# A causal mask added by the matrix engine instead of selected by GpSimd, and another ranking of the work, in a two-layer transformer kernel

## The reference, cut to what matters

```python
q = _rope(q, THETA); k = _rope(k, THETA)
scores = jnp.einsum('bhqd,bhkd->bhqk', q, k) * scale
causal = jnp.tril(jnp.ones((S, S), dtype=bool))
scores = jnp.where(causal[None, None], scores, -jnp.inf)
attn = jax.nn.softmax(scores, axis=-1)
out = jnp.einsum('bhqk,bhkd->bhqd', attn, v)
```

## Time and profile before

| | |
|---|---|
| median of 3 runs | 739.42 us |
| lowest and highest | 735.49, 742.3 us |
| the profiled execution's own time | 740.88 us |
| its span in the profile | 739.1 us |
| mean granted TensorE clock | 0.991 |

### The profile page before, as it was taken

The page is one execution under the profiler, slowest core; times in us unless marked ns, Lnnn a source line. Parts: engine busy times, 40 slices in busy tenths (PEclk is TensorE's granted clock), DMA queues, the critical chain, the costliest instruction groups (busy, mean ns, idle before and its releaser), DMA issues.

```text
span 739.1 us, 15140 instructions
## 1 busy us (share of the span) xinstructions
PE 684.5 (93%) x5750; PEld 506.1 (68%) x5750; DVE 515.2 (70%) x1353; ACT 512.2 (69%) x846; POOL 302.3 (41%) x418
## 2 busy tenths in 40 slices
PE   1879999999999999999999998989999999989996
PEld 1667776878776778777778776655555566666665
DVE  3845455675846665748686856998999898788543
ACT  2867767997778967988777894256575666666861
POOL 2201121122533122212445455675787663544563
PEclk9989999999999999999999999999999999999999
DMA  9100000000020000000011113123333431211011
GB/s 289 61 1 1 0 1 1 0 1 1 1 82 5 1 1 0 1 2 0 1 44 44 43 44 128 44 83 95 110 119 115 148 92 61 95 54 61 2 31 30
DMA packets 40825, 34.98 MB, mean 47 GB/s; under 512 B 2864, under 2 KB 36912, under 8 KB 40496
## 3 DMA queue, kind: packets, MB, share of 16 engines
q1 hardware_dynamic: 40752, 34.00, 14.7%
HBM read 19.05 MB, written 14.68 MB: 46 GB/s over the span
## 4 chain that ended last, share of the span: by engine, by line
PE 59%; DVE 16%; ACT 14%; issue 6%; DMA 3%; POOL 2%; SPq 1%; POOLq 0%; DVEq 0%; ACTq 0%
PE PSA L788 16%; PE PSA L792 15%; DVE MX L1097 5%; PE PSA L960 5%; ACT PSA L1148 3%; PE PSA L805 3%; PE PSA L947 3%; PE PSA L916 2%; DVE G L1020 2%; DMA QS<-dq 2%; PE PSA L901 2%; ACT G L1144 2%; ACT PB L1224 2%; ACT ah L1155 1%; ACT L1144 1%
## 5 line engine op out<-in xcount | busy, mean ns | idle before, releaser
L1247 POOL TENSOR_TENSOR RS<-VE,MHALF 128x4 f32<-128x4 f32 x48 | 49.3, 1028 | 229.9 <-DVE VE L1002 229.8
L788 PE MATMUL PSA<-ah,WH 128*128 128x512 f32 x320 | 131.0, 409 | 6.1 <-DVE al L1025 3.4
L1097 DVE TENSOR_REDUCE MX<-PSA 128x6 f32<-128x768 f32 x128 | 117.6, 949 | 15.2 <-PE PSA L923 14.6
L792 PE MATMUL PSA<-al,WH 128*128 128x512 f32 x320 | 125.2, 391 | 0.0
L1148 ACT ACTIVATE PSA<-PSA,SC 128x512 f32<-128x512 f32 x128 | 84.6, 661 | 57.2 <-PE PSA L792 56.5
L1224 ACT ACTIVATE PB<-PSA 128x768 f32<-128x768 f32 x128 | 100.7, 813 | 18.6 <-PE PSA L947 18.0
L1295 POOL TENSOR_SCALAR_AFFINE_SELECT PB<-PB 128x512 f32<-128x512 f32 x128 | 80.8, 636 | 73.1 <-ACT PB L1224 71.8
L788 PE MATMUL PSA<-bh,WH 128*128 128x512 f32 x256 | 105.7, 413 | 4.0 <-DVE bl L1025 2.5
L792 PE MATMUL PSA<-bl,WH 128*128 128x512 f32 x256 | 101.2, 395 | 0.0
L1025 DVE TENSOR_TENSOR al<-PSA,ah 128x512 fp32r<-128x512 f32 x64 | 44.2, 690 | 68.8 <-ACT ah L1155 68.8
L788 PEld LDWEIGHTS PSA<-ah,WH 128*128 128x128 f32 x320 | 60.1, 188 | 22.6 <-DVE al L1025 5.3
(11 more groups left out here) (123 smaller groups left out, 1416.2 us busy)
## 6 DMA issues: line engine op xcount, KB each, us to landing
KS<-dk SPq DMA_DIRECT2D x32, 192.0 KB
QS<-dq SPq DMA_DIRECT2D x32, 192.0 KB
dk<-CB SPq DMA_DIRECT2D x16, 192.0 KB, 2.3
dq<-CB SPq DMA_DIRECT2D x16, 192.0 KB, 2.3
X<-in_x SPq DMA_DIRECT2D x8, 256.0 KB, 7.2
dk<-CB SPq DMA_DIRECT2D x16, 128.0 KB, 2.0
dq<-CB SPq DMA_DIRECT2D x16, 128.0 KB, 2.0
out<-X SPq DMA_DIRECT2D x8, 256.0 KB, 2.9
```

The lines of the kernel that those rows point to most:

```text
L788: e.matmul(o, WH[:, col:col + 128], hi, start=first, stop=False)
L792: return e.matmul(o, WH[:, col:col + 128], low, start=False, stop=last)
L1097: e.tensor_reduce(MX[:, u % 2, :, :].rearrange("p t (l g) -> p l t g", l=2)[:, :, :, g], PSA[:, b:b + 2, 0:384].rearrange("p l (t k) -> p ...
L1247: e.tensor_tensor(RS[:, i, :], VE[:, i, :], MHALF[:, :], ALU.pow).then_inc(g_rs, 1)
```

## The change

The second passes get their mask the way the first passes have it. Before the scores, four products of `IM` with a new table `ML` (mask halves for keys as rows) write the mask into the banks, and the scores are added on top; the exponential then makes zeros of the masked entries. POOL's select and its semaphore are gone, and `weigh` waits for ACT's exponential itself. The table comes with the same transfer as the others (256 KB become 384 KB), and POOL makes two casts more at the start. In the planner the entry of `pass2` is changed accordingly, and five numbers that rank jobs: the units' attention jobs 6 to 4, `maxima` 5.2 to 1, `fin` 6.6 to 5, the better priority of first passes 5.5 to 5.95, `LEAD` 28 to 32.

```diff
-    "pass2": [("P", 0.18, 0.34), ("A", 0.69, 0.81), ("G", 0.59, 0.63)],
+    "pass2": [("P", 0.34, 0.5), ("A", 0.69, 0.81)],
...
-LEAD = 28
+LEAD = 32
...
-            self.add(6, self.attend(2 * c + h, a, va))
+            self.add(4, self.attend(2 * c + h, a, va))
...
-        return 5.5 if self.count.get("pass1", 0) < self.count.get("pass2", 0) + LEAD else 6.5
+        return 5.95 if self.count.get("pass1", 0) < self.count.get("pass2", 0) + LEAD else 6.5
...
-        self.add(5.2, self.maxima(u, p1))
+        self.add(1, self.maxima(u, p1))
...
-        self.add(6.6, self.fin(u, self.last_weigh))
+        self.add(5, self.fin(u, self.last_weigh))
...
+        ML = sb("ML", [128, 2, 2, 128], BF16)
...
-        MASKS = XP[:, 0, :].rearrange("p (k d) -> p k d", k=4)
+        MASKS = XP[:, :, :].rearrange("p a (k d) -> p (a k) d", k=4)[:, 0:6, :]
...
                     emptied(w, st.emptied)
-                    for k in range(2):
+
+                    for k in (1, 0):
+                        for h in range(2):
+                            e.matmul(PSA[:, b + h, 0:256].rearrange("p (t q) -> p t q", t=2)[:, :, 0:64 + 64 * k],
+                                     IM[64 * h:64 * h + 64, k, :], ML[64 * h:64 * h + 64, k, :, 0:64 + 64 * k],
+                                     start=(k == 1), stop=False, skip_group_check=True)
+                    for k in (1, 0):
                         for h in range(2):
                             o = PSA[:, b + h, 0:384].rearrange("p (t q) -> p t q", t=3)
                             t = e.matmul(o[:, 1, :] if k else o[:, 0::2, :],
                                          K[64 * h:64 * h + 50, g, 128 * k:128 * k + 128],
-                                         Q[64 * h:64 * h + 50, g, 128 * k:256], start=(k == 0), stop=True,
+                                         Q[64 * h:64 * h + 50, g, 128 * k:256], start=False, stop=(k == 0),
                                          skip_group_check=True)
                     t.then_inc(p_pass2, 1)
                 elif st.name == "weigh":
                     V = VA[u % KEPT]
-                    w.wait_ge(g_sel, 8 * u + 2 * g + 2)
+                    w.wait_ge(a_prob, 8 * u + 2 * g + 2)
...
                     for k in range(2):
-                        t = e.tensor_copy(MK[:, :, k, :], MASKS[:, 2:4, :])
+                        e.tensor_copy(MK[:, :, k, :], MASKS[:, 2:4, :])
+                        t = e.tensor_copy(ML[:, :, k, :], MASKS[:, 4:6, :])
...
-                elif st.name == "pass2":
-                    P = PB[:, n % 4, 0:2, :, :].rearrange("p t l q -> p (t l) q")
-                    w.wait_ge(a_prob, n + 1)
-                    e.affine_select(out=P, in_=P, compare_op=ALU.is_ge, fill=0.0, base=0,
-                                    pattern=[[0, 4], [1, 128]], channel_multiplier=-1).then_inc(g_sel, 1)
...
-    arrays["masks"] = np.concatenate([both(np.eye(128, dtype=f32)), both(np.triu(np.full((128, 128), NEG, f32), 1))],
-                                     axis=1)
+    arrays["masks"] = np.concatenate([both(np.eye(128, dtype=f32)), both(np.triu(np.full((128, 128), NEG, f32), 1)),
+                                      both(np.tril(np.full((128, 128), NEG, f32), -1))], axis=1)
```

More of the change, by code:

```diff
@@ L691, in build @@
         v_turn, v_mx, v_peak, v_mt, v_rc = (sem(n) for n in ("v_turn", "v_mx", "v_peak", "v_mt", "v_rc"))
-        g_c, g_rs, g_xn, g_ones, g_wb, g_turn, g_rest, g_sel = (
-            sem(n) for n in ("g_c", "g_rs", "g_xn", "g_ones", "g_wb", "g_turn", "g_rest", "g_sel"))
+        g_c, g_rs, g_xn, g_ones, g_wb, g_turn, g_rest = (
+            sem(n) for n in ("g_c", "g_rs", "g_xn", "g_ones", "g_wb", "g_turn", "g_rest"))
         xin = I["x"].rearrange("b (c p) d -> p (b c) d", p=128)
```

## The result

The changed kernel is slower: 743.02 us (740.26 to 747.36, 9 runs) against 735.49 us (734.06 to 742.3, 9 runs) before, ratio 1.0079 with the 95% interval [1.0047, 1.0111]. On 735.5 us the ratio is 5.8 us. The forecast was a gain of 3.5 us; the time lies in its range, the direction is wrong. The forecast also started from 739.4 us, the median of three runs, where nine runs have 735.5; so the time and the range say less than the difference of the two kernels does.

The account below looks back on a forecast made before the run. DVE's row maxima were taken to bound the attention stage up to 620 us, with PE busy 90.7 of 96.4 us after that. The terms -1 - 3 + 2 - 1.5 = -3.5 us gave 736.5 us, range 727 to 749.

Parts of the forecast that it names:

- The masks' price in the queue: PE's queue, second passes: four mask products take 0.17 us per pass, 128 x 0.17 = 21.8 us.
- These I cost at nothing: Masks of 68 second passes up to 620 us, 11.6 us on PE, cost nothing since DVE is the bound.
- 2 us behind it: Masks of 60 second passes from 620 to 716.4 us, 10.2 us: 2 us of loss, between 0 and 10.2.
- The select's removal: POOL's 128 selects go: 1 us gained on PE's waits, 3 us on DVE instructions blocked beside POOL.
- The peak's three instructions: Small DVE instructions slowed beside POOL: means of some 250 ns expected instead of 276 to 341.
- The very end: Last exponential to last division: ACT's scaling and PE's transposes leave; 1.5 us gained, between 0.7 and 2.0.
- The ranking at 0: Ends of units and pairs come earlier: a move of work, not a saving, costed at 0 before the very end.
- the 5 to 10 expected: Sign on DVE: the last row maximum starts later than 686.4 us by 5 to 10 us.
- the sign of being wrong: The forecast is wrong if the last exponential's end moves more than 6 us either way from 716.4.
- PE becomes the bound: Rival, late stretch: masks stand before scores ACT waits for; +10.2 us gives 749.6, whole queue growth 752.3; chance 0.18.
- POOL was the brake: Rival: PE had room, masks cost nothing, all of 6.3, 2.3 and 2.0 us comes back: 728.8; chance 0.21.
- the ranking costs: Rival: ends moved ahead of the last row maxima load DVE's full stretch, +7 - 3.5, so 743; chance 0.14.

Follow-up runs that it names:

- the half with DVE full: Kernel before without any select, PE mask products for units 0 to 7 only, mask of units 8 to 15 left out: 741.85 us, 1.0025 of before.

## Why the prediction was wrong

- **The masks' price in the queue**, 21.8 us: right. 0.16 to 0.18 us per second pass in the trace, PE busy 12.0 us more, forecast 12.9 with the `keep` products taken off. The 41.5 us estimated from the Trainium skill's figure of about 81 ns per product ("TensorE: Matmul & The Clock Gate", section "Back-to-back issue gap") would have been far too much for this kind of product: the trace after has 40 to 45 ns.
- **"These I cost at nothing" up to 620 us, and 2 us behind it: this step failed.** The two together measured 9.7 us. The forecast set PE's idle time and `keep` products against the masks as one sum of room per stretch. In the old order the half with DVE full cost 6.6 us and the other 7.2, nearly alike, and the mask products hold 6.7% and 11.4% of the chain of waits. Room in the sum was not room at the place: PE works its queue in order, and the mask products stand ahead of first passes that DVE, the full engine, waits for, and ahead of scores that ACT waits for. The `keep` products were at best partly room, since PE's clock fell without them.
- **The select's removal**: forecast 4 us (1 on PE, 3 on DVE), measured 4.8 (2.4 to 7.2) in the old order. The size is right and DVE's busy time did fall by 5.0 us, but not where I said. The peak's three instructions after, and one of the longest beside POOL's line 1293, which runs 1.27 us from 478.10:

```profile
L1114 DVE TENSOR_SCALAR HM<-MX 128x32 bf16<-128x32 f32 x16 | 7.0, 434 | 0.6
L1112 DVE TENSOR_TENSOR MX<-MX 128x16 f32<-128x16 f32 x16 | 4.5, 280 | 0.3
...
L1116 DVE SCALAR_TENSOR_TENSOR HM<-MX,HM 128x32 bf16<-128x32 f32 x16 | 3.4, 210 | 0.6
...
478.11 1.30 DVE L1114 TENSOR_SCALAR HM<-MX 128x32 bf16<-128x32 f32 x1
```

Against the medians of the earlier trace rows they lost 6.1 us after, 6.3 before; means of some 250 ns were forecast and 434, 280 and 210 came. Where they are long now, other work of POOL's stands beside them. The relief came to other DVE instructions: the layer norm's scaling (line 1010 before) took 1.9 us less in all, the steps of lines 1078, 1005, 1002 and 1082 together 4.7. The rule of the Trainium skill ("SBUF — State Buffer", section "Who interferes with whom") that such instructions and GpSimd's shut each other out, and a reduction never takes part, fits both traces; it tells who can be shut out, not how often. The row maxima stayed at a median of 949 ns, as said.
- **The very end**: forecast 1.5 us, measured 1.0. Right.
- **The ranking at 0**: right as the sum needs it without a mask (0.9948 against 0.9935), and wrong as a general statement. It is 11 us better than the old ranking with masks on PE and 12 us worse with the select. I had no term for that interplay. The last row maximum came 10.3 us later, just over the 5 to 10 expected, and the last exponential 6.1 us, just over the 6 that the prediction named as the sign of being wrong.
- **The rivals**: "PE becomes the bound" is what happened, with 98% busy between 620 and 716.4 us and 64 `keep` products left there. Its place was too narrow (both stretches, not the late one alone). Its 10.2 us for the masks are near the 9.7 measured; what it left out was the select's gain of 4.8. "POOL was the brake" had 8.6 us for the select, where 4.8 came, and nothing for the masks, and "the ranking costs" had 7 us for what measured 1.0 without masks. And a change under 1% could be told from none: the interval is 0.3% to either side.

The measured sum: -4.8 for the select, +1.0 for the order without masks (-1.8 to +4.0 from the two kernels' own runs), +9.7 for the masks, +5.9 us; the whole measured +5.8. It closes because it is made of the same ratios; the pieces come from runs on different chips, each against its own runs of before.

Still open: why the new ranking loses 12 us with the select, whether what it gives back with the masks comes from the ranks or from the `keep` products that it does without, which other numbers make up the remaining 4 us, and why a plan that knows of the masks is slower in the old ranking. No kernel tried that has the whole mask beats the kernel before. The two without a mask in the second passes are 0.5 and 0.65% faster, which is about what another way of masking could give in these orders.

## What to carry to other kernels

Don't set an engine's idle time and filler in a stretch against new work as one sum. Where two engines feed each other and one is full, ask what stands behind the new instructions in the queue, for in the old order each microsecond put in front of the full engine's supply cost 0.6. An order laid out by a planner belongs to the kernel it was made for: the same five numbers were worth 11 us in one variant and cost 12 in the other, so a part and its order can only be judged together.

## What the runs showed of the hardware

Products that nobody reads are worth 0.9% in the kernel before: without 378 of them the mean granted clock went from 0.99 to between 0.957 and 0.977. In the changed kernel without 250 of them PE was busy 1.92 of 4 us before the clock fell, in places to 0.50. Four mask products of 64 rows, 768 columns in all, pass through the queue in 0.16 to 0.18 us at a granted clock of 1.00. And taking 80.8 us of one kind of work from POOL did not shorten the small DVE instructions that POOL shuts out at the peak (6.3 us lost before, 6.1 after).
